# A two-layer adaLN network on one core: the second router's low halves on GpSimd, and eight places for the second experts' rows

## The reference, cut to what matters

```python
x = L0_attn_query
h = layernorm(x) * (1 + ca) + sa
x = x + ga * L0_attn(h, ...)        # 16 heads, cumulative sums
h = layernorm(x) * (1 + cb) + sb
x = x + gb * L0_ffn(h, ...)         # 4 experts, the best 2 of each token
h = layernorm(x) * (1 + ca1) + sa1
x = x + ga1 * L1_attn(h, ...)       # 16x16 scores per token group, softmax
h = layernorm(x) * (1 + cb1) + sb1
# L1_ffn: 8 experts, the best 1 of each token
route = sigmoid(h @ Wr + br)        # Wr is 256 x 8
e = argmax(route, axis=1)
x = x + gb1 * max(route) * (gelu(h @ W1[e]) @ W2[e])
```

## Time and profile before

| | us |
|---|---|
| three runs | 1820.65, 1824.22, 1825.49 (median 1824.22) |
| the profiled execution, its own time | 1816.01 |
| its span (first to last instruction) | 1814.2 |

### The profile page before, as it was taken

How to read it: one execution, slowest core, us unless ns; L and a number is a source line. 1 busy time by engine, 2 the same in 40 slices (tenths; PEclk the granted TensorE clock), 3 DMA queues, 4 the chain that set the end, 5 groups by cost and what they waited for, 6 DMA issues and landing times.

```text
span 1814.2 us, 38440 instructions
## 1 busy us (share of the span) xinstructions
PE 1586.2 (87%) x13744; PEld 1176.3 (65%) x13744; DVE 1162.2 (64%) x1812; ACT 904.0 (50%) x2232; POOL 1228.9 (68%) x1009
## 2 busy tenths in 40 slices
PE   6699999987999999999999967878886876599998
PEld 5465656665888788787888852334443425499998
DVE  7778888875444444444445555899999998633333
ACT  6678888742433333343344446544443435454454
POOL 5657777732566666666687735899998995456664
PEclk9899999985999999999999987989998988599999
DMA  6013444336434344444465460001111235288886
GB/s 210 24 44 114 146 142 131 95 135 236 108 95 113 102 107 106 103 109 97 111 172 133 98 196 30 1 26 30 30 42 38 88 115 179 97 276 259 262 260 158
DMA packets 148866, 218.53 MB, mean 120 GB/s; under 512 B 49145, under 2 KB 109201, under 8 KB 143569
## 3 DMA queue, kind: packets, MB, share of 16 engines
q1 hardware_dynamic: 115296, 132.26, 22.8%
q0 software_dynamic: 33392, 83.82, 18.3%
HBM read 144.02 MB, written 72.00 MB: 119 GB/s over the span
## 4 chain that ended last, share of the span: by engine, by line
PE 40%; POOL 28%; issue 15%; DVE 9%; ACT 3%; DMA 2%; POOLq 0%; DVEq 0%; ACTq 0%; SPq 0%
PE ps L774 37%; POOL BIG L2380 13%; POOL XD L2530 5%; DVE BIG L1353 5%; POOL BIG L2541 3%; POOL BIG L2540 3%; POOL BIG L2518 3%; DVE BIG L1901 2%; DMA BIG<-HB,BIG 1%; PE ps L891 1%; ACT BIG L1949 1%; PE ps L1140 0%; DVE BIG L1879 0%; DMA HB<-BIG 0%; ACT BIG L2252 0%
## 5 line engine op out<-in xcount | busy, mean ns | idle before, releaser
L774 PE MATMUL ps<-BIG 128*128 128x256 f16 (+9 forms) x11304 | 1292.2, 287 | 138.9 <-DVE BIG L1879 44.9
L774 PEld LDWEIGHTS ps<-BIG 128*128 128x128 f16 (+3 forms) x11304 | 972.6, 101 | 418.7 <-issue 105.1
L2380 POOL TENSOR_TENSOR BIG<-BIG 128x256 f16<-128x256 f32 (+6 forms) x547 | 739.0, 1386 | 342.9 <-ACT BIG L1949 322.8
L1949 ACT ACTIVATE BIG<-BIG 128x512 f16<-128x512 f32 (+3 forms) x543 | 326.1, 659 | 246.8 <-DVE BIG L1353 190.7
L1353 DVE TENSOR_TENSOR BIG<-BIG 128x512 f16<-128x512 f32 (+10 forms) x343 | 292.5, 862 | 213.9 <-ACT BIG L1949 185.0
L1949 ACT ACTIVATE BIG<-ps 128x64 f32<-128x64 f32 (+6 forms) x687 | 238.4, 419 | 175.6 <-PE ps L1071 88.5
L1353 DVE TENSOR_TENSOR BIG<-ps,BIG 128x512 f32<-128x512 f32 (+2 forms) x389 | 276.8, 773 | 15.8 <-PE ps L774 14.4
L1353 DVE TENSOR_TENSOR BIG<-BIG,ps 128x512 f32<-128x512 f32 (+2 forms) x149 | 98.9, 664 | 246.9 <-PE ps L774 171.8
L1901 DVE TENSOR_REDUCE BIG<-BIG 128x160 f32<-128x2560 f32 x64 | 181.7, 2839 | 0.0
L2518 POOL DMA_INDIRECT BIG<-HB,BIG x109 | 108.6, 996 | 70.3 <-DVE BIG L1353 39.0
L2530 POOL DMA_INDIRECT XD<-BIG x70 | 120.5, 1722 | 28.6 <-issue 14.8
(11 more groups left out here) (149 smaller groups left out, 959.2 us busy)
## 6 DMA issues: line engine op xcount, KB each, us to landing
WD<-BIG SPq DMA_DIRECT2D x80, 256.0 KB
BIG<-in_v SPq DMA_DIRECT2D x32, 512.0 KB
BIG<-in_w SPq DMA_DIRECT2D x24, 512.0 KB
BIG<-WD SPq DMA_DIRECT2D x32, 384.0 KB, 7.8
HB<-BIG SPq DMA_DIRECT2D x64, 128.0 KB, 2.5
WG<-BIG SPq DMA_DIRECT2D x32, 256.0 KB
BIG<-WD SPq DMA_DIRECT2D x16, 512.0 KB, 5.0
XD<-X SPq DMA_DIRECT2D x32, 128.0 KB, 2.5
```

Of the source, the lines that this page charges most:

```text
L774: return e.matmul(o, lhsT, rhs, start=start, stop=stop, skip_group_check=True)
L1949: return e.activation(o, i, ACT.Copy)
L2380: return e.tensor_tensor(o, a, b, op)
```

## The change

Two edits. The low halves of the second router's weights are subtracted by GpSimd, at the end of its step 41, and no longer by VectorE at the end of its step 42. And the ring `HP` of layer 1 has eight places: four new ones lie where the routing buffers will be, tile `i` uses place `(i + 4) % 8`, and the stores of the four new places signal on `ld_x[0]` to `ld_x[3]` (semaphores that had been used for loads of `x` before). The high half of tile `i` now waits for the store and the transposes of tile `i - 8`. Whoever waited for all stores on four semaphores now waits on eight, and VectorE waits for the last stores of the four new places before it adds the bias in `routing(1)`, because the routing buffers overlie these places.

```diff
@@ class Moe
+                if l:
+
+                    self.HP += Area(area.at).ring(4, 2, D, dt=f16)
@@
+        def row_slot(i):
+            return (i + 4) % 8
+
+        def row_stored(i, n):
+
+            k = row_slot(i)
+            return (st_hb[k], 128 + 16 * n) if k < 4 else (ld_x[k - 4], 32 + 16 * n)
+
+        def rows_stored(l):
+            return [row_stored(i, 4) for i in range(8)] if l else [(st_hb[k], 128) for k in range(4)]
@@ SP, rows_out
-                    e.dma_start(M[1].HBv[:, row_tile(1, i), 0:2 * D], M[1].HP[i % 4].rearrange(FLAT)).then_inc(st_hb[i % 4], 16)
+                    e.dma_start(M[1].HBv[:, row_tile(1, i), 0:2 * D], M[1].HP[row_slot(i)].rearrange(FLAT)).then_inc(row_stored(i, 0)[0], 16)
@@ VectorE, routing
+                if l:
+
+                    for i in range(24, 28):
+                        dve.wait_ge(*row_stored(i, 4))
@@ VectorE, routing, second_experts; the same on ScalarE and GpSimd
-                    for k in range(4):
-                        dve.wait_ge(st_hb[k], slot_base[l]["hb"] + 128)
+                    for w in rows_stored(l):
+                        dve.wait_ge(*w)
@@ VectorE, the steps of the attention
-                if q == 42:
-                    router_lo(1)
@@ ScalarE, pre_tick
-                        if i >= 4:
-                            act.wait_ge(st_hb[i % 4], slot_base[l]["hb"] + 16 * (i // 4))
-                            act.wait_ge(s["hT_ps"], at(l, "hT_ps") + i - 3)
-                        copy(m_.HP[i % 4][:, 0, :], m_.HR[i % 4]).then_inc(s["hs_hi"], 1)
+                        if i >= 8:
+                            act.wait_ge(*row_stored(i, i // 8))
+                            act.wait_ge(s["hT_ps"], at(l, "hT_ps") + i - 7)
+                        copy(m_.HP[row_slot(i)][:, 0, :], m_.HR[i % 4]).then_inc(s["hs_hi"], 1)
@@ GpSimd, pre_tick
-                            if i >= 4:
-                                pool.wait_ge(st_hb[i % 4], slot_base[l]["hb"] + 16 * (i // 4))
-                                pool.wait_ge(s["hT_ps"], at(l, "hT_ps") + i - 3)
+                            if i >= 8:
+                                pool.wait_ge(*row_stored(i, i // 8))
+                                pool.wait_ge(s["hT_ps"], at(l, "hT_ps") + i - 7)
@@ GpSimd
+            def router_lo():
+
+                pool.wait_ge(s["rw_hi"], at(1, "rw_hi") + 1)
+                tt(M[1].RW[1].rearrange(FLAT), M[1].RWf.rearrange(FLAT), M[1].RW[0].rearrange(FLAT), ALU.subtract).then_inc(s["rw_lo"], 1)
@@ GpSimd, the steps of the attention
+                if q == 41:
+                    router_lo()
```

More of the change, by code:

```diff
@@ L989, in pre_tick @@
                             pe.wait_ge(s["hT"], at(l, "hT") + i - 1)
-                        flat = m_.HP[i % 4].rearrange(FLAT)
+                        flat = m_.HP[row_slot(i)].rearrange(FLAT)
                         for kk in range(4):
@@ L1526, in vector @@
             heads_lo(NT - 1)
-            def router_lo(l):
-                m_ = M[l]
-                dve.wait_ge(s["rw_hi"], at(l, "rw_hi") + 1)
+            def router_lo():
+                m_ = M[0]
+                dve.wait_ge(s["rw_hi"], 1)
                 tt(m_.RW[1].rearrange(FLAT), m_.RWf.rearrange(FLAT), m_.RW[0].rearrange(FLAT), ALU.subtract).then_inc(s["rw_lo"], 1)
@@ L1541, in vector @@
             rows(27)
-            router_lo(0)
+            router_lo()
             rows_copy(1)
@@ L2214, in second_experts @@
                 act.wait_ge(s["rt"], rt_at[l, "yi"])
-                for k in range(4):
-                    act.wait_ge(st_hb[k], slot_base[l]["hb"] + 128)
+                for w in rows_stored(l):
+                    act.wait_ge(*w)
                 turn(0)
@@ L2482, in pre_tick @@
                     if st == 2:
-                        hp = m_.HP[i % 4]
+                        hp = m_.HP[row_slot(i)]
                         if row_by_pool(l, i):
                             pool.wait_ge(s["hr"], at(l, "hr") + 2 * i + 2)
-                            if i >= 4:
-                                pool.wait_ge(st_hb[i % 4], slot_base[l]["hb"] + 16 * (i // 4))
-                                pool.wait_ge(s["hT_ps"], at(l, "hT_ps") + i - 3)
+                            if i >= 8:
+                                pool.wait_ge(*row_stored(i, i // 8))
+                                pool.wait_ge(s["hT_ps"], at(l, "hT_ps") + i - 7)
                             e.tensor_copy(hp[:, 0, :], m_.HR[i % 4]).then_inc(s["hs_hp"], 1)
@@ L2581, in second_experts @@
                 fetch_weights(0)
-                for r in range(4):
-                    pool.wait_ge(st_hb[r], slot_base[1]["hb"] + 128)
+                for w in rows_stored(1):
+                    pool.wait_ge(*w)
                 fetch(1, 0)
```

## The result

| | median us | runs |
|---|---|---|
| before | 1823.84 | 1820.65 to 1825.49, 4 runs |
| after | 1809.68 | 1806.67 to 1812.34, 4 runs |

The ratio is 0.9915 (95% interval 0.9897 to 0.9934): 14.2 us off the medians, where 12.7 were forecast (1811.5). Measured again on another chip, the changed kernel stood at 0.9923 (0.9898 to 0.9948) of before. So the change is faster, and the size forecast lies inside the interval, which in microseconds is 12.0 to 18.8.

What follows compares the result with a forecast made beforehand. GpSimd was taken to set the pace in most of layer 1's attention, other engines in the rows. Gains of 8.9 and 3.8 sum to 12.7 us, from 1824.2 to 1811.5; range 1809 to 1814, with two rivals 1804 to 1816.5.

Steps and rivals of the forecast that it cites:

- part 1: Layer 1's attention: moving the router's subtraction to GpSimd removes the long chunk's excess, 8.9 us, between 7.6 and 10.2.
- two undisturbed chunks: Attention: one long and one short chunk take 93.5 us, against 102.66 with the stall, so 9.2 us go.
- The price of the added one: Attention: GpSimd's new 128x16 subtraction lies on the path and costs 0.25 us, between 0.15 and 0.31.
- its wait for `rw_hi` is free: GpSimd, step 41: ScalarE's copy comes in step 40, before powers that GpSimd has already waited for; no added wait.
- Rival D: Attention: the block is mutual, GpSimd's subtraction waits for a VectorE pause, up to 40 us; 1831.3 at 20; chance 0.02.
- part 2: Rows' stage: eight places remove ScalarE's waits for row stores, 3.8 us, from 2.6 to 7.5.
- the start of TensorE's stretch: Rows, tile 5: without the wait for tile 1's store TensorE resumes 2.2 us earlier, between 1.8 and 2.3.
- it is not shortened: Rows: the stretch that TensorE bounds, 11.79 busy of 12.00 us, only begins 2.2 earlier and keeps its length.
- The middle: Rows, 1540 to 1557 us: VectorE is the next bound once the store waits go, so only 0.4 us comes back.
- The end: Rows, tile 30: ScalarE's idle time before the last two tiles is uncovered; 1.35 us, between 1.0 and 1.5.
- the 3 to 5 that I named as its sign: Rows' stage in the profile after: 3 to 5 us shorter, a sign that the eight places work as forecast.
- The added waits: Before the bias addition: four more store waits, already met, cost 0.1 to 0.2 us; 0.15 in the sum.

Runs made afterwards that it cites:

- the part alone: For part 1: kernel before with only the subtraction moved to GpSimd, 0.9949. For part 2: changed kernel with the subtraction back on VectorE in step 42, 0.9971.
- The kernels of the last comparison: On one chip: kernel before, 1779.51 us; the kernel cut at nine; changed kernel with old waits back for tiles 4-7, 16-23 or 24-31, 1768.0, 1764.3, 1770.0 us.
- the kernel cut at nine: Changed kernel, subtraction on VectorE after the steps, VectorE multiplying nine of the second half's sixteen heads, GpSimd seven (before eight each): 1755.91 us, 0.9870.

## Why the prediction was right, and where it was not

**The long chunk, part 1: right in mechanism and size.** Forecast 8.9 us (7.6 to 10.2); the part alone measured 9.3 (6.4 to 12.3), and the two chunks fell from 102.6 to 102.9 down to 93.5 to 95.6. Over the whole attention the traces give 7.7, the low end of the range: 93.5 us for two undisturbed chunks, one of each form, was too little, as the long form is the commoner one. What carried it was to take the excess of the chunk over its neighbours and not the length of the stalled instruction. The price of the added one, 0.25 us, was 0.24 to 0.26. The step that its wait for `rw_hi` is free held (idle before it 0.0).

**That GpSimd runs on unhindered: right.** Rival D needed a block of GpSimd by VectorE; there is none in any trace with the subtraction on GpSimd. These traces have no long VectorE instruction with two SBUF inputs in the steps, so whether such a one would block GpSimd stays untested.

**The rows, part 2: right in mechanism, a size off.** Forecast 3.8 us, with 7.5 as the upper bound; the stage shrank by 5.9 in the traces and the part alone by 5.3 in time. By its terms: the start of TensorE's stretch, 2.2, measured 2.15. But "it is not shortened" failed: the stretch from TensorE's return to its last early transposes is 0.7 us shorter, for the same 138 matmuls (busy time by stretches, the kernel before, columns as in the earlier trace rows):

```profile
1527.78:1540.04 12.26, 12.05 (x138) 10.80 (x138) 7.19 (x17) 8.30 (x24) 5.62 (x10) 0.86 0.80 264
```

the same view of the changed kernel:

```profile
1523.97:1535.51 11.54, 11.54 (x138) 10.46 (x138) 8.26 (x21) 8.41 (x24) 5.41 (x9) 0.87 0.95 290
```

0.2 us of it were waits (12.05 busy of 12.26, against all of 11.54), the rest is less busy time for the same work. All of it lies in the first 4.6 us: from there on both stretches take 7.68 us (1532.36 to 1540.04, 1527.83 to 1535.51). A part is the clock: transposes of four blocks take 0.59 to 0.61 us at the lower of the two clock levels (1.2 GHz) and 0.38 at the higher, and the lower one lasted until about 3.3 us into the stretch before and 2.9 after. By these lengths that is worth 0.1 to 0.2 us, an estimate; what made the other 0.3 is not shown. The middle, 0.4, measured 0.6. The end, 1.35, measured 2.5 (6.55 to 4.09), and the experiments say which part is whose: 1.4 to 1.6 by the wait of the last tiles, about as forecast, and 0.8 to 1.0 by the waits of the middle tiles. That is the term that was mis-sized: I let VectorE cover the middle waits, 15.87 busy of 17.10 us, and counted what VectorE could win. VectorE did cover most of them while it had tiles to make. But ScalarE and GpSimd had fallen behind under it, and after VectorE's last tile there was no cover left for what they owed. VectorE's idle time before the bias addition fell to 3.1 us and not to about 4.2, and the stage itself, 5.9 us shorter, is outside the 3 to 5 that I named as its sign and above the 5 that my range counts for this part, for which the prediction gives no reason beside its own upper bound of 7.5.

**The added waits: right.** Nothing in the trace after waits for a store before the bias addition, which starts 0.05 us after the end of the last logits (1555.09 and 1554.72 + 0.32), where it was 0.04 before. The 0.15 us that I gave them did not show: in the trace the four waits are two more instructions of VectorE's sequencer, the last of them over 1.5 us before the bias addition.

**The time.** The sum of the terms was 1.5 us under the measured gain, less than the interval can tell (12.0 to 18.8). By the traces it is made of two errors that partly cancel: part 1 worth 7.7 and not 8.9, part 2 worth 5.9 and not 3.8, together 13.6. That the total came so near is in part luck. Carrying the 8.2 us between the profiled execution and the median over unchanged was harmless, though the traces show that such a difference arises mostly in the stages before and behind the change (1165 to 1177 us to the second chunk, 251.6 to 260.3 behind the bias addition, on those chips).

## What to carry to other kernels

An instruction that is nearly 70 times longer than its sister of nearly the same shape is a wait that the profile can't name: look at what the other engines do over exactly its length, and in particular at GpSimd when the slow one is VectorE's with two SBUF inputs; put such an instruction where GpSimd rests, or on GpSimd, or give it one input from PSUM. When the stalled engine doesn't set the pace, the gain is the excess of the period over its neighbours, not the stall. And a wait covered by a busy third engine is not free if the waiting engines must finish after it: count it again at the tail.

## What the runs showed of the hardware that was not expected

VectorE's stall does not end at the end of a GpSimd instruction but of a run of them: 5.3, 10.2, 10.6 and twice 10.8 us, each to within 0.04 us of GpSimd's first rest, past five starts of GpSimd instructions (three in the shortest).

The kernels of the last comparison ran on a chip on which all of them, before included, are some 50 us faster (before: 1779.51 us there, 1829.61 and 1828.08 on two others). Most of it is made by the end of the first experts: the second chunk of layer 1's attention starts at 1124 to 1127 us in the four traces from it and at 1165 to 1177 in the others. One stretch of 100 us of that stage, first the changed kernel on a slower chip (busy time by stretches, columns as in the earlier trace rows):

```profile
580.00:680.00 100.00, 92.83 (x855) 80.94 (x854) 43.44 (x56) 36.27 (x55) 65.53 (x52) 1.00 0.44 108
```

Then the kernel cut at nine on this one:

```profile
580.00:680.00 100.00, 100.00 (x942) 89.91 (x940) 39.76 (x62) 41.69 (x64) 69.32 (x56) 1.00 0.47 115
```

TensorE is granted the full clock in both, but on the slower chip it does 855 matmuls where the other does 942, and stands still in between for no releaser that the trace can name, as in this line of TensorE in order of time:

```profile
809.95 2.23 PE L789 MATMUL ps<-BIG 128*128 x19 [1.05 <-issue]
```

Between 555 and 1060 such pauses of over 0.2 us add up to 24 to 29 us in the ten traces from the slower chips, and to none in the four from this one, which is more than half of the difference at the second chunk. What they are stays open; ratios are taken on one chip each and don't feel them.
